# A perceiver layer on one core: identity products at both ends, the gate's reciprocal in two pieces, the context's lower parts on POOL, and new orders

## What is computed

```python
x = x + xattn(layernorm(x), ctx)      # layernorm again, 16 heads of 64, softmax over 257 keys, @ Wo + bo
x = x + attn(layernorm(x))            # layernorm again, 16 heads of 16 over 32 tokens, @ W_proj + b_proj
x = x + ffn(layernorm(x))             # x_prev = x shifted by one token
# ffn: xr, xk = mixes of x and x_prev;  r = sigmoid(xr @ W_r.T);  out = r * (relu(xk @ W_k.T)**2 @ W_v.T)
```

## Time and profile before

| | |
|---|---|
| median of 3 runs | 888.02 us (887.44 to 891.44) |
| the profiled execution, its own time | 890.68 us |
| its span in the trace | 888.6 us |
| PE busy | 811.1 us, 91% |
| DVE, ACT, POOL busy | 612.1, 598.0, 414.6 us |
| granted clock of PE, mean | 0.972 |
| DMA | 30.51 MB, mean 34 GB/s |

### The profile page before, as it was taken

How to read it: one execution, slowest core, us unless ns; L and a number is a source line. 1 busy time by engine, 2 the same in 40 slices (tenths; PEclk the granted TensorE clock), 3 DMA queues, 4 the chain that set the end, 5 groups by cost and what they waited for, 6 DMA issues and landing times.

```text
span 888.6 us, 20369 instructions
## 1 busy us (share of the span) xinstructions
PE 811.1 (91%) x7279; PEld 662.5 (75%) x7279; DVE 612.1 (69%) x1857; ACT 598.0 (67%) x1423; POOL 414.6 (47%) x664
## 2 busy tenths in 40 slices
PE   5698989999999999999999999999999989788865
PEld 3477768897798869886788869886888767577643
...
PEclk9899999999999999999999999999999999999956
...
GB/s 216 120 13 37 25 61 13 26 26 25 49 16 34 25 60 14 25 25 39 35 25 25 25 61 13 26 25 67 8 25 25 37 37 12 13 26 16 11 1 13
DMA packets 49523, 30.51 MB, mean 34 GB/s; under 512 B 22928, under 2 KB 48336, under 8 KB 49424
## 3 DMA queue, kind: packets, MB, share of 16 engines
...
## 4 chain that ended last, share of the span: by engine, by line
PE 72%; DVE 13%; ACT 6%; issue 5%; SPq 1%; DMA 1%; POOL 1%; POOLq 0%; DVEq 0%; ACTq 0%
PE score L786 15%; PE post L872 5%; PE pre L671 5%; PE probT L797 5%; DVE qk_t L1270 4%; PE aux L730 3%; PE post L881 3%; PE ac_main L812 2%; PE ac_main L817 2%; PE ac_tail L818 2%; PE ac_tail L814 2%; PE ac_main L813 2%; DVE qk_l L1265 2%; PE post L852 2%; PE post L858 2%
## 5 line engine op out<-in xcount | busy, mean ns | idle before, releaser
L428 POOL TENSOR_TENSOR prT_l<-prT,prT_h 128x512 fp32r<-128x512 f32 x128 | 170.9, 1339 | 137.6 <-ACT prT_h L1066 137.0
L571 POOL TENSOR_SCALAR pr<-pr,rsum,poison 128x257 f32<-128x257 f32 x256 | 145.4, 578 | 187.1 <-DVE rsum L1295 186.7
L1289 DVE CUSTOM_DVE_ANT_0 sm<-score,mbias 128x257 f32<-128x257 f32 x256 | 108.1, 424 | 97.5 <-PE score L786 82.0
L1047 ACT ACTIVATE pr<-sm,nmx 128x257 f32<-128x257 f32 x256 | 129.2, 506 | 44.9 <-DVE nmx L1289 43.4
L786 PE MATMUL score<-cT_h,qk_h 128*128 128x258 f32 x256 | 92.5, 361 | 15.7 <-DVE qk_t L1270 11.4
L1055 ACT ACTIVATE prT<-probT 128x512 f32<-128x512 f32 x128 | 75.8, 592 | 23.7 <-PE probT L797 22.5
L1066 ACT ACTIVATE prT_h<-prT 128x512 fp32r<-128x512 f32 x128 | 79.5, 628 | 11.5 <-PE ac_tail L818 10.8
L797 PE MATMUL probT<-ident,pr 128*128 128x128 f32 x512 | 78.4, 276 | 4.3 <-POOL pr L571 3.9
L786 PE MATMUL score<-cT_h,qk_t 128*128 128x258 f32 x256 | 73.1, 286 | 0.0
L786 PE MATMUL score<-cT_l,qk_h 128*128 128x258 f32 x256 | 72.9, 285 | 0.0
L786 PE MATMUL score<-cT_h,qk_l 128*128 128x258 f32 x256 | 72.8, 284 | 0.0
...
## 6 DMA issues: line engine op xcount, KB each, us to landing
...
```

What stands on the lines that cost most here:

```text
L428: eng.tensor_tensor(prT_l[:, :, cut], prT[:, :, cut], prT_h[:, :, cut], ALU.subtract).then_inc(prob_lower, 1)
L571: last = pool.tensor_scalar(p, p, rsum[:, j % 2, t:t + 1], poison[:, 0:1], ALU.mult, ALU.mult)
L1047: act.activation(pr[j % 2][:, t, :], sm[:, t % 2, :], ACT.Exp, bias=nmx[:, j % 2, t:t + 1], scale=-1.0, accum_out=ssum[:, j % 2, t:t + 1]) ...
L1289: dve.tensor_tensor_reduce(sm[:, t % 2, :], score[t % 2][:, 0:NK], mbias[:], DH ** -0.5, BIG, ALU.add, ALU.min, nmx[:, j % 2, t:t + 1]).th ...
```

## The change

1. PE begins with WARM: 18 products of the identity with itself, 128x128, into a bank that nobody reads; then XT, before the key weights' transposes. LEFT moves up between WK1 and WK2, into another bank, and so waits until DVE has copied WK1.
2. In the closing 21 products Z0 to Z20 (`keep_clock`, identity with 256 columns of wo, into aux) stand between the jobs; aux is taken out of the banks of the closing's second half.
3. The loads of gamma, beta, the last context rows and the mask (8 DMAs) move from SP's queue to ACT's.
4. CL runs on POOL in place of DVE.
5. SG is in two pieces of 128x256, SG0 and SG1, with other jobs between them.
6. The `alone` increments are gone.
7. All twelve tables are in another order.

Cut to its core (the other tables change as the two shown do):

```diff
 PE_FIRST = (
-    "H0 G2 H2 S0:0 H4 H6 CT:1 G3 H8 H10 S1:0 S2:0 LV0 S3:0 CT:2 S0:1 P0:0 S1:1 LV1 P1:0 S2:1 S3:1 CT:3 F0 S0:2 S1:2 S2:2 "
+    "G2 H0 H2 H4 CT:1 G3 H6 S0:0 H8 CT:2 S1:0 H10 S2:0 S3:0 S0:1 S1:1 P0:0 S2:1 LV0 S3:1 CT:3 P1:0 LV1 S0:2 F0 S1:2 S2:2 "
...
 PE_LAST = (
...
+    "FR FK P1:6 S3:7 FV LT.0 AC:6 OT0.0 P0:7 OT1.0 LT.1 P1:7 WO.0 AC:7 OT0.1 T2.0 OT1.1 QT.0 KT.0 WO.1 Z0 SC.0 VR.0 Z1 Z2 "
+    "Z3 T2.1 QT.1 KT.1 Z4 Z5 Z6 Z7 Z8 SC.1 VR.1 PT.0 PV.0 Z9 T4.0 Z10 Z11 PJ.0 PT.1 PV.1 T4.1 Z12 PJ.1 Z13 Z14 T3.0 Z15 "
+    "T3.1 FR.0 FK.0 FR.1 FK.1 Z16 FV.0 Z17 Z18 Z19 Z20 FV.1").split()
...
-SETUP = "WK0 WK1 XT WK2 WK3 Q0 LEFT Q1 CT0".split()
+SETUP = "WARM XT WK0 WK1 LEFT WK2 WK3 Q0 Q1 CT0".split()
+N_WARM = 18
+N_SETUP_KEYS = (2, 4, 4, 4, 4, 4)
...
+FILL = tuple(f"Z{n}" for n in range(21))
...
-LOWER_ON_DVE = ("CL",)
+LOWER_ON_DVE = ()
...
-        CLOSING_BANKS = [(pre, post), (ac_main, aux, score[0], score[1], probT, ac_tail)]
-        wk_bank, left_bank = [ac_main, ac_tail, aux, post], score[0]
+        CLOSING_BANKS = [(pre, post), (ac_main, score[0], score[1], probT, ac_tail)]
+        wk_bank, left_bank = [ac_main, ac_tail, aux, post], ac_tail
+        warm_bank = score[0]
...
-        def alone(eng):
-
-            eng.sem_inc(waits_passed)
-
...
             sp.dma_start(xn[:], token_rows(x_rows, 0)).then_inc(x_in, 16)
-            for n, v in ((G1, g1), (B1, be1)):
-                sp.dma_start(cols[:, n, :], column(v)).then_inc(ln1_in, 16)
             sp.dma_start(wk_main, Wkv[0:P, 0:NH * DH]).then_inc(wk_staged, 16)
...
-            sp.dma_start(left_in[:, 0:DC], ctx_in[:, NKF, :]).then_inc(left_staged, 16)
-            sp.dma_start(left_in[:, DC:256], ctx_in[:, NKF, P:DC]).then_inc(left_staged, 16)
             load_ctx(0, 0)
-            for r in range(4):
-                sp.dma_start(mraw[r * NQ:(r + 1) * NQ, :], mask[0, 0, :, :]).then_inc(mask_in, 16)
...
                 pool.wait_ge(recip_done, 2 * (g * GB + j) + half + 1)
-                alone(pool)
...
-                    after(pe, setup_copied, min(int(name[1]), 2))
+                    after(pe, setup_copied, (0, 1, 2, 2)[int(name[1])])
+                    if name == "Q2":
+                        pe.wait_ge(left_split, 1)
...
-                    pe.wait_ge(setup_copied, N_SETUP)
+                    pe.wait_ge(setup_copied, N_SETUP_KEYS[d])
...
+            def keep_clock():
+
+                pe.matmul(aux[:, 0:256], ident[:], wo[:, 0, :], start=True, stop=True)
+
             def run():
                 for name, g, j in stream(PE_STREAM):
-                    if name[0] == "H":
+                    if name in FILL:
+                        keep_clock()
+                    elif name[0] == "H":
                         qk_job(int(name[1:]), 0)
...
+                elif name == "WARM":
+                    for _ in range(N_WARM):
+                        pe.matmul(warm_bank[:, 0:P], ident[:], ident[:], start=True, stop=True)
                 elif name == "LEFT":
                     pe.wait_ge(left_staged, 32)
+                    pe.wait_ge(setup_copied, 2)
...
+            for n, v in ((G1, g1), (B1, be1)):
+                act.dma_start(cols[:, n, :], column(v)).then_inc(ln1_in, 16)
+            act.dma_start(left_in[:, 0:DC], ctx_in[:, NKF, :]).then_inc(left_staged, 16)
+            act.dma_start(left_in[:, DC:256], ctx_in[:, NKF, P:DC]).then_inc(left_staged, 16)
+            for r in range(4):
+                act.dma_start(mraw[r * NQ:(r + 1) * NQ, :], mask[0, 0, :, :]).then_inc(mask_in, 16)
...
-                    elif base == "SG":
-
+                    elif base in ("SG", "SG0", "SG1"):
+
+                        nth_part = nth_half if a is not None else int(base[2])
+                        mine = gate if a is not None else gate[:, nth_part * DM:(nth_part + 1) * DM]
                         dve.wait_ge(er_exp, g + nth_half + 1)
-                        dve.tensor_scalar(gate, gate, 1.0, None, ALU.add).then_inc(er_one, 1)
-                        dve.wait_ge(er_one, g + nth_half + 1)
-                        dve.reciprocal(gate, gate).then_inc(r_ready, 1)
+                        dve.tensor_scalar(mine, mine, 1.0, None, ALU.add).then_inc(er_one, 1)
+                        dve.wait_ge(er_one, 2 * g + nth_part + 1)
+                        dve.reciprocal(mine, mine).then_inc(r_ready, 1)
```

More of the change, by code:

```diff
@@ new lines @@
+    "T3.1 FR.0 FK.0 FR.1 FK.1 Z16 FV.0 Z17 Z18 Z19 Z20 FV.1").split()
+ACT_FIRST = (
[4 rows of a table added]
+    "F2 S3:7 U0:6 U1:6 CU:7 AC:5 K2 P0:7 K3 K4 P1:7 K5 K6 AC:6 K7 U0:7 K8 U1:7 CT:0 K9 K10 K11 AC:7").split()
+ACT_ORDER = (
[4 rows of a table added]
+    "CU:7 U1:6 AC:5 K0 K1 K2 K3 P0:7 U0:7 AC:6 K4 K5 P1:7 U1:7 K6 CT:0 K7 LV1 K8 K9 K10 K11 AC:7").split()
+ACT_LAST = (
[5 rows of a table added]
+    "T4.1 T3.0 M0.0 T3.1 M0.1 FK.0 EZ.0 FK.1 EZ.1").split()
+DVE_FIRST = (
[3 rows of a table added]
+    "AC:4 R1:6 R0:7 S2:7 S3:7 R1:7 K0 K1 AC:5 K2 K3 LT K4 K5 K6 AC:6 K7 K8 CT:0 K9 K10 K11 AC:7").split()
@@ L120 @@
+DVE_ORDER = (
[4 rows of a table added]
+    "R0:7 SG1 R1:7 FV AC:5 K0 K1 K2 K3 LT K4 K5 AC:6 K6 CT:0 K7 K8 K9 K10 K11 AC:7").split()
+DVE_LAST = (
[7 rows of a table added]
+    "FV.1").split()
 POOL_FIRST = (
-    "CT:1 N0:0 CT:2 N1:0 L0:0 N0:1 N1:1 L1:0 CT:3 N0:2 N1:2 CT:4 L0:1 L1:1 N0:3 L0:2 L1:2 N1:3 N0:4 CT:5 L0:3 N1:4 L1:3 "
-    "CT:6 N0:5 CT:7 L0:4 L1:4 N1:5 N0:6 L0:5 LX N1:6 L1:5 N0:7 N1:7 L0:6 L1:6 L0:7 L1:7 CT:0").split()
+    "CL:0 CL:1 N0:0 CT:1 L0:0 CT:2 N1:0 L1:0 N0:1 CT:3 N1:1 N0:2 N1:2 CL:2 L0:1 L1:1 CT:4 N0:3 CT:5 L0:2 LX N1:3 L1:2 "
+    "L0:3 CL:3 L1:3 N0:4 CT:6 N1:4 CL:4 L0:4 L1:4 N0:5 N1:5 CT:7 CT:0 CL:5 N0:6 L0:5 N1:6 N0:7 L1:5 N1:7 L0:6 L1:6 CL:6 "
+    "CL:7 L0:7 L1:7").split()
@@ L123 @@
 POOL_ORDER = (
-    "CT:1 XB N0:0 CT:2 N1:0 L0:0 L1:0 N0:1 N1:1 CT:3 X1 N0:2 L0:1 L1:1 N1:2 CT:4 N0:3 L0:2 L1:2 N1:3 W0 W1 L0:3 N0:4 CT:5 "
-    "L1:3 N1:4 CT:6 L0:4 N0:5 CT:7 L1:4 N1:5 N0:6 L0:5 LX L1:5 N1:6 KA L0:6 L1:6 N0:7 N1:7 YO CT:0 L0:7 L1:7").split()
+    "N0:0 CT:1 CT:2 XB CL:0 N1:0 L0:0 N0:1 L1:0 N1:1 X1 CT:3 CL:1 N0:2 L0:1 L1:1 N1:2 CL:2 L0:2 L1:2 N0:3 CT:4 W0 N1:3 "
+    "CT:5 W1 CL:3 L0:3 N0:4 L1:3 CT:6 N1:4 CL:4 N0:5 L0:4 CT:7 L1:4 N1:5 N0:6 L0:5 N1:6 CL:5 L1:5 KA CL:6 N0:7 L0:6 L1:6 "
@@ L126 @@
+    "LX N1:7 CT:0 L0:7 CL:7 L1:7 YO").split()
 POOL_LAST = (
-    "CT:1 N0:0 XB CT:2 N1:0 N0:1 L0:0 L1:0 N1:1 CT:3 L0:1 N0:2 X1 N1:2 L1:1 CT:4 L0:2 W0 N0:3 N1:3 L1:2 W1 N0:4 L0:3 CT:5 "
-    "L1:3 N1:4 CT:6 N0:5 CT:7 L0:4 N1:5 L1:4 N0:6 LX L0:5 N1:6 L1:5 N0:7 L0:6 L1:6 KA N1:7 YO L0:7 L1:7 XB.0 X1.0 W.0 "
-    "X1.1 W.1 KA.0 CT:0 KA.1 YO.0 YO.1").split()
-SETUP = "WK0 WK1 XT WK2 WK3 Q0 LEFT Q1 CT0".split()
+    "CT:1 XB N0:0 CT:2 CL:0 LX N1:0 L0:0 L1:0 N0:1 CT:3 N1:1 CT:4 N0:2 CL:1 L0:1 X1 N1:2 CT:5 L1:1 N0:3 CL:2 L0:2 L1:2 "
@@ L133 @@
+    "CL:3 W0 N1:3 N0:4 L0:3 W1 N1:4 CT:6 L1:3 CL:4 L0:4 CT:7 N0:5 L1:4 N1:5 N0:6 L0:5 CL:5 L1:5 CL:6 N1:6 L0:6 KA L1:6 YO "
+    "N0:7 N1:7 XB.0 CL:7 L0:7 L1:7 X1.0 W.0 X1.1 W.1 KA.0 KA.1 YO.0 YO.1 CT:0").split()
+SETUP = "WARM XT WK0 WK1 LEFT WK2 WK3 Q0 Q1 CT0".split()
+N_WARM = 18
+N_SETUP_KEYS = (2, 4, 4, 4, 4, 4)
 QK_NEEDS = ("Q0", "Q1", "Q1", "Q2", "Q3", "Q3")
@@ L629, in run @@
                         job(name, g)
-            pool.wait_ge(setup_copied, N_SETUP)
+            pool.wait_ge(left_split, 1)
             pool.wait_ge(consts_made, 8)
@@ L985, in _ @@
                         last = pe.transpose(wk_bank[n][:, i * DC + P:(i + 1) * DC], wk_tail[:, pair], ident[0:64, 0:64])
-                    last.then_inc(setup_full, 1)
+                    last.then_inc(keys_full, 1)
+                elif name == "WARM":
+                    for _ in range(N_WARM):
+                        pe.matmul(warm_bank[:, 0:P], ident[:], ident[:], start=True, stop=True)
                 elif name == "LEFT":
                     pe.wait_ge(left_staged, 32)
+                    pe.wait_ge(setup_copied, 2)
                     pe.transpose(left_bank[:, 0:NB], left_in[:, 0:P], ident[0:NB, 0:NB])
-                    pe.transpose(left_bank[:, NB:2 * NB], left_in[:, P:256], ident[0:NB, 0:NB]).then_inc(setup_full, 1)
+                    pe.transpose(left_bank[:, NB:2 * NB], left_in[:, P:256], ident[0:NB, 0:NB]).then_inc(left_full, 1)
                 elif name == "CT0":
@@ L1185, in run, with column @@
                         post_job(name, g)
+            def column(v):
+                return v.rearrange("(k p) -> p k", p=P)
+            for n, v in ((G1, g1), (B1, be1)):
[4 more added lines that the diff above has]
+                act.dma_start(mraw[r * NQ:(r + 1) * NQ, :], mask[0, 0, :, :]).then_inc(mask_in, 16)
             act.wait_ge(ident_made, 2)
@@ L1224, in layer_norm @@
                 elif stage == 1:
-                    alone(dve)
                     for a in part:
```

27 lines of the change are left out of this document (10 added, 17 removed), and 72 rows, old and new, of tables (ACT_FIRST, ACT_LAST, ACT_ORDER, DVE_FIRST).

## The result

| | median | all runs | ratio to before, 95% interval |
|---|---|---|---|
| before | 888.96 us | 887.44 to 891.44 | |
| after the change | 876.63 us | 875.55 to 877.46 | 0.9858 [0.9831, 0.9885] |

The change makes the kernel 1.4% faster, 12.3 us, where 20 were forecast. The profiled execution of after took 877.46 us.

The account below looks back on a forecast made before the run. PE, busy 91% of the span, was taken as the bound, with time to win at the ends. Gains of 4 + 0.5 + 5.5 + 2 + 1 + 7 = 20 us took the profiled 890.7 to 870.7, as median 868 us; range 858 to 881.5.

Parts of the forecast that it names:

- WARM and the setup: Kernel start: products raise PE's clock early, LEFT's wait costs about 1 us; net gain 4 us.
- first rival's first place: Setup: Q0 and Q1 run slow again after the transposes, costing 3.5 us; the rival as a whole had 0.19.
- Order of the first group: First group: jobs put ahead of S0:0 fill PE's waits and avoid half speed; gain 5.5 us, between 0 and 9.5.
- Loads on ACT's queue: Setup: key weights' loads start 1 us earlier, part lost to busy DMA engines; gain 0.5 us, between 0 and 1.
- CL to POOL: POOL takes CL at 1.1 us a batch, standing at 55%; nil in the middle groups, 2 us gained in the last.
- SG in pieces: Gate's reciprocal on DVE: no wait behind a piece over 1.7 us; PE did not stop for it, gain 0.
- Increments: Dropped semaphore steps sit behind waits of engines with slack; between 0 and 1 us for all, taken as 0.
- Middle orders: Middle groups: new table orders gain 1 us for all groups, between -6 and +6.
- The closing: Closing: full clock saves 10 us, fillers cost 3; net gain 7 us, between -3 and +10.
- clock rival: Clock does not hold in setup (3.5 us) or closing (10 us); 881.5 us with both, 878 with closing alone; chance 0.19.
- taken back in the middle: Rival: new orders put a 0.3 us wait in every batch, 19 us in all; time 887 us; chance 0.06.
- POOL did not become the bound: Denies the rival that late CL on POOL makes PE wait; 900 us at 0.5 us a batch; chance 0.05.

Follow-up runs that it names:

- e3: The changed kernel without the 18 WARM products at its start: 878.10 us, ratio 0.9908.
- e1: The changed kernel with SP's 16 DMAs of the last values issued in two halves, eight after each copy: 869.76 us, ratio 0.9805.
- e6: e1 with ten more identity products between the transposes of the setup: 868.12 us, ratio 0.9782.
- e2: The changed kernel with the first group's four tables as before, and that group's CL on DVE: 871.24 us, ratio 0.9819.
- e5: The changed kernel with the edits of e1 and e2 together: 871.12 us, ratio 0.9816.
- e11: e6 with 13 identity products in the first group, nine ahead of S2:0 and four ahead of S3:0: 867.11 us, ratio 0.9760.
- e7: The changed kernel with the gate's reciprocal whole again, at the place of SG0: 884.66 us, ratio 0.9969.
- e10: The kernel before with only the gate's reciprocal cut in two pieces, the second placed later: 900.47 us, ratio 1.0119.
- e9: The changed kernel with the `alone` increments put back at their six places: 878.88 us, ratio 0.9891.
- e4: The changed kernel without the 21 filler products Z0 to Z20 of the closing: 878.66 us, ratio 0.9916.

## Why the prediction was right and where it failed

The direction held, and 876.63 us lies inside the range. The forecast 868 was 8.6 us too low. By its steps:

- **WARM and the setup, net 4.** The mechanism of WARM was right to a tenth (end at 7.6 us, XT at 8.22 in 0.66 us). LEFT's wait was 0.81 us, where about 1 was taken. What WARM bought was 1.0 to 2.5 us (e3 at S2:0), and the whole setup was 1.2 us ahead of before at Q1's end in after and 2.7 in e1 (20.2 and 18.8 us for 21.5), not 4: the first rival's first place happened. Ahead of Q0 came only transposes and LEFT's wait, and the clock fell. e6 holds it, but the products that hold it took back what Q0 and Q1 gained.
- **Order of the first group, 5.5.** This term failed. It was reckoned from the waits ahead of S0:0 and S2:0, and S2:0 did come 7.3 us earlier. But the text had itself named what is late next, SP's queue, at 1 to 4 us, and then left it out of the sum. It came to a wait of 4.23 us in place of 1.17 in before, and to more behind it, since the clock went with it: e1 gives 5.4 to 6.2 us back. And the term took a lead at S2:0 for a lead at the end of the group. The order has the first, 5.0 us without e1's edit (42.3 in e2) and 7.4 with it, but of these 7.4 only 1.6 are left at the first WO0 (e1 against e5), which one trace each can't tell from nothing.
- **Loads on ACT's queue, 0.5.** No run had it alone.
- **CL to POOL, last group 2.** Sizes on POOL, 64 of each; the rows of after:

```profile
L430 POOL TENSOR_TENSOR prT_l<-prT,prT_h 128x512 fp32r<-128x512 f32 x128 | 165.1, 1292 | 89.9 <-ACT prT_h L1070 89.2
...
L422 POOL TENSOR_TENSOR c_hl<-cx_in,c_hl 128x256 fp32r<-128x256 f32 x64 | 46.9, 733 | 0.0
...
L421 POOL TENSOR_TENSOR c_hl<-cx_in,c_hl 128x128 fp32r<-128x128 f32 x64 | 31.0, 484 | 18.6 <-ACT c_hl L1077 18.6
```

  733 + 484 = 1217 ns a batch, where 1.1 us was taken, and POOL is at 55% as forecast. The last group gained 3.5 us (4.7 to 5.0 in e1 to e6 and e11, which have its code there), for which the gate's pieces and the new order stand as well as CL.
- **SG in pieces, 0.** This term failed too, to the other side. "PE did not stop for it in the middle" was read from the old order, where the old tables had been laid around the whole reciprocal. In the new order the cut is worth 7.3 us in the middle and last group (e7), in the old one less than nothing (e10). A row of before can't price a part of a change whose order is found together with it.
- **Increments, 0 with a bound of 1 us.** 2.4 us in the middle groups (e9). The bound was too tight.
- **Middle orders, 1.** The middle gained 4.4 us, for everything together. It fell within the 6 us that were kept for it. By taking them out, the pieces are worth 7.2 us and the increments 2.4 in this stretch, more than the whole gain. Either these parts don't add up, or the new order and CL on POOL cost some 5 us there; no run tells which. PE waits in the named places as long as before (0.79 us ahead of S0:0, 0.81 then). Over the four groups between the second WO0 and the sixth PE's busy time is 384.3 of 393.3 us for 386.1 of 395.6, so 1.8 of these 2.3 us lie inside what counts as busy. What made it shorter no row shows.
- **The closing, 7.** 7.4 measured: 2.9 from the fillers (e4), the other 4.5 from orders, banks and chance of the clock. The sum had it the other way round, 10 from the clock less 3 for the fillers. The clock still fell twice.
- **The rivals.** The clock rival was half true: its first place came, its second only for some 7 of the last 20 us in which PE worked. On balance nothing was taken back in the middle. POOL did not become the bound: PE's longest wait for `pr` in the last group was 2.5 us, 2.13 before.
